# Expert networks in half-array tiles, with gate rows spread from DRAM

## The chip, the cores and the metric

The kernel runs on one core of one Trainium2 chip. The metric is the device time of one execution in microseconds (us), taken as the median of several runs. The engines are TensorE (PE in the profile, its weight loads PEld), VectorE (DVE), ScalarE (ACT), GpSimd (POOL) and SyncE (SP), whose queue issues the DMAs here.

## The reference

Input is `x` of 8 images, 64 channels, 16 by 16 pixels. Every layer adds its result to a running sum. A deformable 3x3 convolution and a second convolution come first; then, on 2048 tokens of 64 channels (8 images of 256 tokens): causal attention with 8 heads, a mixture of experts, a windowed attention, and a second mixture of experts. The two that the change touches, cut to what matters:

```python
# T: running sum, 2048 tokens x 64; y = layernorm(T) before each of them
# experts 2: E=8, hidden 256, top 2 of 8 experts per token
h = gelu(y @ W1[e] + b1[e]);           T += sum_e gate2[t, e] * (h @ W2[e] + b2[e])
# windowed attention over 16 tokens (needs its own layernorm), then
# experts 3: E=16, hidden 128, top 2 of 16
h = silu(y @ w1[e]) * (y @ w2[e]);     T += sum_e gate3[t, e] * (h @ w3[e])
```

All experts are computed for all tokens; `gate2` and `gate3` are zero but for a token's two best experts.

## The kernel before, in words

It is written engine by engine, one instruction stream each, with semaphores between them, and every stream has its order written out by hand. Tokens lie in 16 tiles of 128; four tiles make a chunk `c` of 512 tokens (`CHUNK`, `CW`). The stages in order are the convolutions, 64 attention steps (`scores`, `normalise`, with the fills of `attention_fills`), 64 steps of experts 2 and 64 steps of experts 3.

Layernorm output is kept as two float32r numbers, high and low part, whose sum is y. `Y2` holds both beside each other (64 + 64 columns), `transpose_y` turns them, and `ln_evac` puts them into `YTs`: partitions 0 to 63 the high part, 64 to 127 the low part, columns the tokens. The first-layer weights are split the same way: `WH` and `WL`, each with the same 64 rows twice. So two float32r matmuls of 128 rows, one with `WH` and one with `WL` (lines 1608 and 1659), give the full-precision product for 128 hidden units and 512 tokens.

Experts 2: step n makes one bank of 128 hidden units (L1608); ScalarE applies Gelu (L743) into `hid`; two steps later four float32 matmuls (L1627), one for each 128 tokens, take `hid` as the stationary operand and 64 columns of `W2` as the moving one, so that outputs have tokens on partitions. Line 1622 first puts the bias `b2` into the banks. Four experts (`UNIT`) of one chunk share two banks; `combine` (L1168) multiplies them by the gates, which are then plain per-token numbers, and GpSimd adds the four experts up by halving (`fold_unit`, `fold`, L513) and adds to `T` (L516).

Experts 3: each step makes two banks (L1659), ScalarE applies Silu to one (L753), VectorE multiplies by the other (L1258), and L1644 makes the output as above.

All other TensorE work of these stages (transposes of y, small projections for gates and window attention, the window sums, result transposes) is a "fill": `FIRST_FILLS` and `SECOND_FILLS` say after which step each comes, and they share one bank, number 7, which must be free (`misc_free`) before the next. VectorE does the layernorms (`ln_center`, `ln_variance`, `ln_out`), the gates (`take_logits`, `top_first`, `top_second`, `top_gate`), the window attention and most evacuations of bank 7; GpSimd also raises to powers (`ln_power`, `top_power`, `z_power`).

## Time and profile before

| what | value |
|---|---|
| median of 3 runs | 520.0 us (518.88 to 523.47) |
| profiled execution | 519.7 us, its span 517.9 us |
| TensorE clock granted, mean | 0.98 |
| PE busy | 476.3 us (92%) |
| VectorE busy | 360.5 us (70%) |
| ScalarE busy | 266.5 us (51%) |
| GpSimd busy | 170.8 us (33%) |
| the chain that ended last | PE 70%, DVE 20%, ACT 4%, issue 4% |

The span runs from the first to the last instruction; 1.8 us of the execution lie outside it. A float32 matmul stands in the profile as two records, a float32r matmul or a transpose as one. Durations of matmuls overlap, so what one costs is read from the distance between starts.

### The profile page before, as it was taken

The numbers are of one execution on the slowest core, as the hardware profiler recorded it, in microseconds if no ns is written. First come the engines' busy times: TensorE is split into PE (matmuls) and PEld (weight loads), VectorE is DVE, ScalarE is ACT, GpSimd is POOL, SyncE is SP. The second block draws the span as 40 slices with busy tenths as digits, with TensorE's granted clock in tenths as the row PEclk, the third lists the DMA queues.
The fourth block names the chain that finished last, engine by engine and source line by source line (L and its number), as shares of the span: only waits on it lengthen the run. The fifth ranks groups of instructions, "written<-read, shape, count | busy, mean of one in ns | idle before, by whom it ended". The sixth has DMA issues, their size and how long they took to land.

```text
span 517.9 us, 9531 instructions
## 1 busy us (share of the span) xinstructions
PE 476.3 (92%) x3406; PEld 408.0 (79%) x3406; DVE 360.5 (70%) x1050; ACT 266.5 (51%) x631; POOL 170.8 (33%) x217
## 2 busy tenths in 40 slices
PE   2998999959889999999999999999999989989994
PEld 2686787724449898899998998999999878878893
DVE  3288777368857768979797544366577998786844
ACT  1478666521328887888897544444443223322330
POOL 4800000001314493671133324033354434434332
PEclk9999999979979999999999999999999999999997
DMA  8200000000120303000000000000000000000000
GB/s 194 104 2 1 2 1 1 1 0 1 34 47 3 82 4 80 1 1 1 2 2 2 1 1 1 1 1 1 1 1 1 0 3 1 0 14 9 1 11 10
DMA packets 5458, 8.14 MB, mean 16 GB/s; under 512 B 2850, under 2 KB 4514, under 8 KB 4900
## 3 DMA queue, kind: packets, MB, share of 16 engines
q1 hardware_dynamic: 5268, 7.43, 5.9%
q8 instruction: 27, 0.44, 0.4%
q14 instruction: 19, 0.16, 0.1%
q10 hardware_dynamic: 144, 0.11, 0.1%
HBM read 7.01 MB, written 0.52 MB: 15 GB/s over the span
## 4 chain that ended last, share of the span: by engine, by line
PE 70%; DVE 20%; ACT 4%; issue 4%; DMA 1%; SPq 0%; DVEq 0%; ACTq 0%
PE PS L1659 11%; PE PS L1627 10%; PE PS L1644 9%; PE PS L1368 6%; PE PS L1608 6%; PE PS L1384 6%; PE PS L1532 4%; PE PS L1544 3%; DVE M L934 2%; PE PS L1329 2%; PE PS L1560 2%; PE PS L1561 2%; PE PS L1472 2%; ACT score_arena L721 2%; PE PS L1476 1%
## 5 line engine op out<-in xcount | busy, mean ns | idle before, releaser
L513 POOL TENSOR_TENSOR pr<-pr 128x512 f32<-128x512 f32 (+2 forms) x70 | 67.2, 961 | 108.6 <-DVE pr L1032 37.2
L753 ACT ACTIVATE VV<-PS 128x512 f32<-128x512 f32 x64 | 38.2, 597 | 86.8 <-PE PS L1659 86.8
L1627 PEld LDWEIGHTS PS<-wk,hid 128*128 128x128 f32 x512 | 66.6, 191 | 6.4 <-ACT hid L743 1.2
L1644 PEld LDWEIGHTS PS<-wk,hid 128*128 128x128 f32 x512 | 66.9, 191 | 5.6
L743 ACT ACTIVATE hid<-PS,wk 128x512 f32<-128x512 f32 x64 | 43.8, 687 | 49.2 <-PE PS L1608 49.2
L1627 PE MATMUL PS<-wk,hid 128*128 128x64 f32 x512 | 63.9, 268 | 0.7 <-ACT hid L743 0.7
L1644 PE MATMUL PS<-wk,hid 128*128 128x64 f32 x512 | 64.1, 268 | 0.0
L721 ACT ACTIVATE score_arena<-score_arena,nmx 128x128 f32<-128x128 f32 (+1 forms) x128 | 56.9, 447 | 13.6 <-DVE nmx L1127 13.0
L1258 DVE TENSOR_TENSOR hid<-VV,PS 128x512 f32<-128x512 f32 x64 | 43.8, 686 | 23.2 <-PE PS L1659 16.7
L1659 PE MATMUL PS<-YTs,WH 128*128 128x512 f32 x128 | 57.6, 450 | 1.9 <-DVE hid L1258 1.8
L1659 PE MATMUL PS<-YTs,WL 128*128 128x512 f32 x128 | 50.5, 395 | 0.0
L662 ACT ACTIVATE st_mem<-PS 128x512 f32<-128x512 f32 x72 | 36.5, 615 | 21.6 <-PE PS L1384 21.6
L887 DVE TENSOR_TENSOR prod<-hats 128x768 f32<-128x768 f32 x48 | 42.5, 951 | 0.1
L1532 PE MATMUL PS<-YTs,QH 128*128 128x128 f32 (+1 forms) x128 | 38.3, 323 | 0.0
L1544 PE MATMUL PS<-cst,score_arena 128*128 128x128 f32 x192 | 33.0, 280 | 4.7 <-ACT score_arena L721 4.2
L1384 PEld LDWEIGHTS PS<-cst,prod 128*128 128x128 f32 x288 | 31.3, 141 | 7.1 <-issue 3.5
L1384 PE MATMUL PS<-cst,prod 128*128 128x128 f32 x288 | 34.1, 275 | 2.8 <-DVE prod L887 1.9
L1168 DVE TENSOR_TENSOR pr<-PS,gate 128x512 f32<-128x512 f32 x48 | 30.8, 684 | 7.6 <-PE PS L1627 6.4
L1532 PE MATMUL PS<-YTs,QL 128*128 128x128 f32 (+1 forms) x128 | 36.0, 282 | 0.0
L490 POOL TENSOR_TENSOR lnst<-lnst,cst 128x4 f32<-128x4 f32 x16 | 16.3, 1022 | 55.5 <-DVE lnst L977 55.3
L1368 PE MATMUL PS<-st_mem,U 128*64 128x256 f32 x288 | 33.5, 383 | 0.0
L1019 DVE TENSOR_TENSOR QL<-PS,QH 128x512 fp32r<-128x512 f32 x32 | 22.0, 689 | 13.7 <-ACT QH L698 13.7
(225 smaller groups left out, 1065.4 us busy)
## 6 DMA issues: line engine op xcount, KB each, us to landing
stage<-in_wexp SPq DMA_DIRECT2D x6, 512.0 KB, 5.9
wk<-in_w SPq DMA_DIRECT2D x1, 1032.0 KB, 8.5
wa<-in_wat SPq DMA_DIRECT2D x1, 768.0 KB, 6.8
cst<-in_consts SPq DMA_DIRECT2D x1, 580.0 KB, 6.7
X<-in_x SPq DMA_DIRECT2D x2, 256.0 KB, 5.3
out<-X SPq DMA_DIRECT2D x16, 32.0 KB, 1.9
wc<-in_w SPq DMA_DIRECT2D x2, 183.5 KB, 6.2
score_arena<-in_wcv SPq DMA_DIRECT2D x2, 144.0 KB, 6.5
```

Source lines behind the costliest of these rows:

```text
L513: step(nc.gpsimd.tensor_tensor(buf[:, :, 0:width], buf[:, :, 0:width], buf[:, :, width:2 * width], ALU.add))
L721: ins = nc.scalar.activation(PR[:, s % 3, cols], MS[:, s % 3, cols], ACT.Exp, bias=nmx[:, s % 3, qt:qt + 1], scale=-1.0, accum_out=rsum[:, ...
L743: nc.scalar.activation(hid[:, n % 3], PS[:, n % 3, :], ACT.Gelu, bias=wk[:, W128["b1"]][:, e2:e2 + 1]).then_inc(gelu_done, 1)
L887: nc.vector.tensor_tensor(prods[unit % 2][:, b].rearrange("p k (a b) -> p k a b", a=HH), hk[:, 0].unsqueeze(3).to_broadcast([P, TRIPLE, HH ...
L1258: nc.vector.tensor_tensor(hid[:, n % 3], sil[:, n % 2], PS[:, (2 * n + 1) % 3, :], ALU.mult).then_inc(prod3_done, 1)
L1368: ins = mm(PS[h * C:(h + 1) * C, 5 + j % 2, 0:S], U[:, 4 * j + 2 * qt + h, k * C:(k + 1) * C], ST[:, v % ST_TAPS, h, qt], start=(k + qt == ...
L1384: ins = nc.tensor.transpose(PS[:, T_BANKS[m % 6], (2 * qt + pt) * P:(2 * qt + pt + 1) * P], prods[i // TRIPLE % 2][:, 2 * pt + h, k % TRIP ...
L1532: ins = mm(PS[:, s % 2, cols], w[:, a % 2, g, qt * P:(qt + 1) * P], YTs[:, a * S:a * S + (qt + 1) * P], start=(r == 0), stop=(r == 1))
L1544: ins = nc.tensor.transpose(PS[:, 3 + v % 2, k * P:(k + 1) * P], PR[:, v % 3, k * P:(k + 1) * P], ident)
L1627: ins = mm(accumulator(u, q, e % UNIT), hid[:, v % 3, q * P:(q + 1) * P], wk[:, W128["w2_2"]][:, r * C:(r + 1) * C], start=False, stop=(v ...
L1644: ins = mm(accumulator(u, q, e % UNIT), hid[:, v % 3, q * P:(q + 1) * P], wk[:, W128["w3"]][:, e * C:(e + 1) * C], start=True, stop=True)
L1659: ins = mm(PS[:, (2 * n + a) % 3, :], w[:, 1 + a, e * P:(e + 1) * P], YTs[:, c * CW:(c + 1) * CW], start=(k == 0), stop=(k == 1))
```

## The change

1. Output products of the experts. The stationary operand is now the 64 columns of `W2` or `w3`, the moving one is all of `hid` (512 tokens). Two experts are worked on as a pair: one writes PSUM partitions 0 to 63, the other 64 to 127 of the same bank (two 64-column tiles of the array). Outputs have channels on partitions and tokens along the bank. A pair of one chunk is a unit: 16 of experts 2, 32 of experts 3.
2. Input products. Three float32r products with 64 rows each (high by high, low weight by high y, high weight by low y) take the place of two with 128 rows; the two members of a pair use rows 0 to 63 and 64 to 127 (`split_pair`). For this a second transposed copy `YX` with the halves swapped is made: `Y2` gets a third block, `zB` and `zD` are its transposes.
3. Gates. Since tokens now run along the bank, the gate row of an expert must stand on 64 partitions. `gate_turn` turns the gates of a chunk (fills `tB`, `tD`), ScalarE copies them to `gate_rows`, SP stores them in DRAM, and for every unit SP reads the two rows back, each to 64 partitions (`gate_wide`, four slots).
4. Sums. `combine` handles one bank per unit (for experts 2 it also adds `b2`), GpSimd adds it to `acc` with one instruction, and once for each chunk and layer `token_sum` (fills `fC`, `fE`) turns the sum back to tokens and adds both halves; VectorE adds that to `T`.
5. Moves. Most evacuations of bank 7, the rounding to the high part and the output copies go from VectorE to ScalarE, the scaling by 1/sigma in these stages from VectorE to GpSimd. The bias matmuls go. `hid` has four slots in the room of `stage`. A step (q in experts 2, r in experts 3) now does a pair, so there are 32 of each. Fills and side work are put at new steps.

```diff
+            def split_pair(banks, m, tiles, c):
+                cs = slice(c * CW, (c + 1) * CW)
+                for k, (w, ys) in enumerate(((WH, (YTs, YX)), (WL, (YTs, YX)), (WH, (YX, YTs)))):
+                    for i in range(2):
+                        hs = slice(i * C, (i + 1) * C)
+                        ins = mm(PS[:, banks[i], :], w[hs, m, tiles[i] * P:(tiles[i] + 1) * P], ys[i][hs, cs], start=(k == 0), stop=(k == 2))
+                return ins
+            def first_out(q):
+                u, ht = divmod(q, 2)
+                if ht == 0 and u >= 3:
+                    pe.wait_ge(combined, u - 2)
+                pe.wait_ge(gelu_done, 2 * q + 2)
+                for i in range(2):
+                    r = tile2(u, 2 * ht + i)
+                    ins = mm(PS[i * C:(i + 1) * C, OUT_BANKS[u % 3], :], wk[:, W128["w2_2"]][:, r * C:(r + 1) * C],
+                             hid[:, (2 * q + i) % 4], start=(ht == 0), stop=(ht == 1))
+                ins.then_inc(out2_done, 1)
+            for q in range(2 * UNITS2):
...
+                if q >= 2:
+                    pe.wait_ge(gelu_done, 2 * q - 2)
...
+                split_pair([HID_BANKS[(2 * q + i) % 4] for i in range(2)], 0, [tile2(u, 2 * ht + i) for i in range(2)], c).then_inc(hid2_ready, 1)
+                if q >= 1:
+                    first_out(q - 1)
+                for what in FIRST_FILLS.get(q, ()):
+                    more(what)
+            for r in range(UNITS3):
...
+                for a in range(2):
+                    if r == 0:
+                        pe.wait_ge(gelu_done, 4 * UNITS2 - 1 + a)
+                    elif a == 0:
+                        pe.wait_ge(silu_done, 2 * r)
+                    else:
+                        pe.wait_ge(prod3_done, 2 * r)
+                    split_pair([HID_BANKS[2 * i + a] for i in range(2)], 1 + a, [2 * p + i for i in range(2)], c).then_inc(hid3_ready, 1)
+                if r >= 1:
+                    second_out(r - 1)
```

The gate path, on SP, TensorE and VectorE:

```diff
+            for u in range(UNITS2 + UNITS3):
+                m, c, p = unit_of(u)
+                if p == 0:
+                    E = (E2, E3)[m]
+                    sp.wait_ge(misc_free, FILL[("tB", "tD")[m], c] + 1)
+                    sp.dma_start(gate_store[m, c, 0:E], gate_rows[0:E, c % 2]).then_inc(gate_stored, 16)
+                    sp.wait_ge(gate_stored, 16 * (4 * m + c + 1))
+                if u >= WIDE:
+                    sp.wait_ge(combined, u - WIDE + 1)
+                for i in range(2):
+                    sp.dma_start(gate_wide[i * C:(i + 1) * C, u % WIDE, :],
+                                 gate_store[m, c, 2 * p + i:2 * p + i + 1, :].to_broadcast([C, CW])).then_inc(gate_spread[u % WIDE], 16)
+                if u >= UNITS2 + PAIRS3 and p == STORE_AT:
+                    store(c - 1)
...
+                dve.wait_ge(gate_spread[u % WIDE], 32 * (u // WIDE + 1))
+                if u >= 2:
+                    dve.wait_ge(acc_added, added(u - 1))
+                to = weighted[:, u % 2] if p else acc[:, c % 2]
...
+            def gate_turn(name, c):
+                m, E = (0, E2) if name == "tB" else (1, E3)
+                pe.wait_ge(gate_ready, 4 * m + c + 1)
+                take(name, c)
+                for q in range(CHUNK):
+                    ins = mm(PS[0:E, 7, q * P:(q + 1) * P], gate[:, m, 4 * c + q, 0:E], ident, start=True, stop=True)
+                ins.then_inc(misc_filled, 1)
+            def token_sum(name, c):
...
+                for q in range(CHUNK):
+                    ins = mm(PS[:, 7, q * C:(q + 1) * C], acc[:, c % 2, q * P:(q + 1) * P], c_("halves"), start=True, stop=not late)
```

The fills at their new steps:

```diff
+FIRST_FILLS = {0: (("zB", 2),), 1: (("tB", 0),), 2: (("tB", 1),), 4: (("tB", 2),), 5: (("yB", 3),), 6: (("gB", 3),), 7: (("zB", 3),),
+               10: (("fC", 0),), 13: (("yC", 0),), 14: (("pC", 0),), 16: (("tB", 3),), 18: (("wC", 0),), 19: (("fC", 1),),
+               21: (("yD", 0),), 22: (("gD", 0),), 23: (("yC", 1),), 24: (("pC", 1),), 25: (("zD", 0),), 26: (("fC", 2),),
+               28: (("wC", 1),), 29: (("tD", 0),), 31: (("yD", 1),)}
+SECOND_FILLS = {0: (("gD", 1),), 1: (("yC", 2),), 2: (("pC", 2),), 3: (("zD", 1), ("fC", 3)), 5: (("wC", 2),), 6: (("tD", 1),),
+                8: (("yD", 2),), 9: (("gD", 2),), 10: (("zD", 2),), 11: (("yC", 3),), 12: (("pC", 3),), 13: (("tD", 2), ("fE", 0)),
+                14: (("oT", 0),), 15: (("wC", 3),), 19: (("yD", 3),), 20: (("gD", 3),), 21: (("zD", 3), ("fE", 1)), 22: (("oT", 1),),
+                23: (("tD", 3),), 27: (("fE", 2),), 29: (("oT", 2),)}
```

In ScalarE's stream of experts 2, `y_high` (which waits for GpSimd's scaling) stands after the seventh Gelu (n = 6), then after n = 25, 41, 45 and 60.

## Rows read from the trace of the kernel before

**Rows 1.** The page, its second part: GB/s in 40 slices of 12.9 us.

```profile
GB/s 194 104 2 1 2 1 1 1 0 1 34 47 3 82 4 80 1 1 1 2 2 2 1 1 1 1 1 1 1 1 1 0 3 1 0 14 9 1 11 10
```

**Rows 2.** Stages: us, then PE, PEld, DVE, ACT, POOL busy (count), clock, DMA.

```profile
141.00:282.20 141.20, 133.41 (x1053) 121.99 (x1053) 110.15 (x435) 111.33 (x369) 59.45 (x89) 0.98 0.10 23
282.20:379.30 97.10, 95.63 (x702) 88.94 (x701) 51.24 (x139) 46.73 (x68) 33.16 (x35) 1.00 0.01 1
379.30:509.50 130.20, 125.53 (x829) 110.82 (x827) 101.84 (x218) 38.75 (x66) 53.64 (x57) 1.00 0.02 4
509.50:517.90 8.40, 0.81 (x4) 0.29 (x2) 3.25 (x6) 0.00 (x0) 0.00 (x0) 0.61 0.07 16
```

**Rows 3.** The chain that ended last, in order of time: start, us, what.

```profile
311.44 0.84 PE PS L1627 x8
312.80 0.84 PE PS L1627 x8
...
397.85 0.84 PE PS L1644 x8
398.69 0.98 PE PS L1659 x4
399.67 0.84 PE PS L1644 x8
```

**Rows 4.** Timeline of PE: float32r matmuls of 512 columns, and one fill.

```profile
342.64 0.61 PE L1459 MATMUL PS<-cst,Y 128*128 128x128 f32 x4
343.01 0.47 PE L1608 MATMUL PS<-YTs,WH 128*128 128x512 f32 x1
...
379.33 0.48 PE L1659 MATMUL PS<-YTs,WH 128*128 128x512 f32 x1
379.65 0.40 PE L1659 MATMUL PS<-YTs,WL 128*128 128x512 f32 x1
379.89 0.39 PE L1659 MATMUL PS<-YTs,WH 128*128 128x512 f32 x1
```

**Rows 5.** Timeline: float32 matmuls, in 64-column tiles (128*64) and in the whole array.

```profile
83.46 2.36 PEld L1368 LDWEIGHTS PS<-st_mem,U 128*64 128x64 f32 x24 [0.17 <-issue]
83.46 2.81 PE L1368 MATMUL PS<-st_mem,U 128*64 128x256 f32 x24
86.20 2.84 PE L1384 MATMUL PS<-cst,prod 128*128 128x128 f32 x24
...
132.61 7.13 PE L1316 MATMUL PS<-cst 128*128 128x512 f32 x16
```

**Rows 6.** Timeline of PE: float32r matmuls of 288 columns in 64-row tiles.

```profile
25.88 0.29 PE L1356 MATMUL PS<-DH,GL 64*128 64x288 f32 x1
25.99 0.29 PE L1356 MATMUL PS<-DL,GH 64*128 64x288 f32 x1
26.01 0.29 PE L1356 MATMUL PS<-DH,GL 64*128 64x288 f32 x1
26.12 0.29 PE L1356 MATMUL PS<-DL,GH 64*128 64x288 f32 x1
```

**Rows 7.** Groups of DVE instructions from 379.3 us on: count, busy, mean ns.

```profile
L1258 DVE TENSOR_TENSOR hid<-VV,PS 128x512 f32<-128x512 f32 x64 | 43.8, 686 | 23.2 <-PE PS L1659 16.7 <-issue 3.8 <-ACT VV L753 2.4
L1168 DVE TENSOR_TENSOR pr<-PS,gate 128x512 f32<-128x512 f32 x34 | 21.8, 683 | 2.3 <-PE PS L1644 1.2 <-PE PS L1627 1.1
L998 DVE CAST YTs<-PS 128x512 fp32r<-128x512 f32 x5 | 3.4, 682 | 0.0
```

**Rows 8.** Timeline at the start of experts 2: chunk 3's layernorm.

```profile
291.54 0.17 DVE L977 TENSOR_SCALAR lnst<-lnst 128x4 f32<-128x4 f32 x1
...
291.79 1.01 POOL L490 TENSOR_TENSOR lnst<-lnst,cst 128x4 f32<-128x4 f32 x1 [3.38 <-DVE lnst L977]
```

**Rows 9.** The page: two groups of ACT instructions.

```profile
L743 ACT ACTIVATE hid<-PS,wk 128x512 f32<-128x512 f32 x64 | 43.8, 687 | 49.2 <-PE PS L1608 49.2
...
L662 ACT ACTIVATE st_mem<-PS 128x512 f32<-128x512 f32 x72 | 36.5, 615 | 21.6 <-PE PS L1384 21.6
```

**Rows 10.** The page: DMA issues, KB each, median us to landing.

```profile
out<-X SPq DMA_DIRECT2D x16, 32.0 KB, 1.9
...
rw<-in_rows ACTq DMA_DIRECT2D x1, 103.0 KB, 4.0
```

**Rows 11.** Timeline of the end.

```profile
509.66 1.29 DVE L1168 TENSOR_TENSOR pr<-PS,gate 128x512 f32<-128x512 f32 x2 [1.20 <-PE PS L1644]
...
513.37 0.42 DVE L1251 COPY X<-PS 128x256 f32<-128x256 f32 x1 [0.78 <-PE PS L1503]
513.82 2.38 SPq L413 DMA_DIRECT2D out<-X  x4
```

## What the change will do to the time

> **What bounds the kernel now.** I read the stages first [rows 2]. TensorE is busy for 95.6 of the 97.1 us of experts 2 and for 125.5 of the 130.2 us of experts 3; VectorE for 51.2 and 101.8. The clock is granted in full (1.00, the 2.4 GHz level) in both. The chain that ended last says the same: it walks from one TensorE step to the next, every 1.36 us in experts 2 and every 1.82 us in experts 3 [rows 3]. A step's output part takes 0.84 us: eight records, each waiting for a weight load of 128 columns, though it streams only 64. Then the input part: a float32r matmul of 512 columns starts 0.234 us after the one before it, 0.31 us where it follows the float32 ones [rows 4]. So 64 x 1.36 = 87 us and 64 x 1.82 = 116 us are these steps; fills, bias matmuls and a few waits make the other 10 and 14 us. The profiled execution is 519.7 us for a span of 517.9, against a median of 520.0; I sum against the span and add 1.8 us.
>
> **Output products.** A float32 matmul is two records, and one record of 512 columns takes 7.13/16 = 0.44 us, less its tail 0.427, thus two 2.4 GHz cycles for a column [rows 5]. A pair has two matmuls, four records: 1.7 us if one after another, no better than now (two steps, 1.68 us). Do the column tiles overlap? L1368 is this form: 24 records of 256 columns, 0.213 us each by that rate, would be 5.1 us; they took 2.74 us to the next group's start [rows 5]. So two run at once: 12 x 0.216 = 2.59 us, and 0.15 us is the change of tiling at the ends. A pair's output is then 2 x 0.432 = 0.86 us.
>
> The Trainium skill speaks against this here (TensorE: Matmul & The Clock Gate, Part 3, The mechanism): a weight load overlaps running matmuls only where its row group differs, and column tiles share all rows. By it the four 64-column loads of a pair would stand on the path. The trace disagrees: the 24 loads of L1368 lie inside its matmuls.
>
> **Input products.** Three double matmuls take the place of two single ones per member. In 64-row tiles L1356 shows two streams, each with a start every 0.13 us for 288 columns (0.12 by 2.4 GHz), interleaved 0.02 us apart [rows 6]; so two at once again. For 512 columns I take 0.234 us per double: 0.70 us for a pair, against four matmuls, 0.94 us, now.
>
> **Changes of tiling.** Each step goes from row tiles to column tiles and back. From the same rows I take 0.15 us for each change, 0.30 us a step (between 0.1, which is only the late start, and 0.5, if the first weights can't be loaded early).
>
> **TensorE, summed.** Experts 2: 0.70 + 0.86 + 0.30 = 1.87 us a step, x32 = 60 us (87 before). Experts 3: 1.40 + 0.86 + 0.30 = 2.57 us, x32 = 82 us (116 before). The fills grow. A transposing fill cost 0.37 us and more to the next start [rows 4]; with the change of tiling 0.55. In experts 2 there are 8 of these (4.4 us), 5 gate turns of eight records like 128-column transposes, 0.9 us each (4.5), 3 sums of eight 128-column loads, 0.95 (2.9), and 6 small ones (3.0): 15 us. In experts 3: 7 transposes, 3 turns, 4 sums, and 10 small ones: also 15 us. The bias matmuls go. TensorE alone thus needs 75 and 97 us.
>
> **Experts 2, what is late next.** ScalarE: 64 x 0.687 = 44 us of Gelu [rows 9], 12 bank copies at 0.6 like L662 [rows 9], 5 roundings and two tanh: 55 us of 80, busy but not the bound; a step's two Gelus (1.4 us) must end in the 1.87 us until TensorE's output part, so a copy between them costs some tenths unless a fill lies there too. One wait is plain: the seventh Gelu is followed by a rounding that needs chunk 3's layernorm. L977 ends at 291.7 us, the power on GpSimd at 292.8 [rows 8], the scaling (new there, about 0.75) at 293.6. ScalarE would reach this place at about 291.6, and the eighth Gelu and TensorE's output part queue behind it: some 2.5 us. Later, chunk 0's and chunk 1's second layernorms end about 1 us behind the fills that need them, and the Gelu table comes at the start: 4 us together. 75 + 2.5 + 4 = 81 us, against 97.1.
>
> **Experts 3, what is late next.** VectorE. A step has two products (0.686 each) and one combine of the same size [rows 7]: 2.1 us with gaps. Of its 101.8 us now, products and combines are 65.6; of the other 36.2 us the copies out of bank 7, the scalings, the roundings, the final halving and one layernorm (12 us) leave this engine or stage; 5 sums add 2.1 us. That leaves 26 us, and about 100 short waits between dependent ones make it 31. All but 0.5 us of it lies in steps 0 to 22. The second input pair of a step waits for both products of the step before, so a step lasts as long as the longer of TensorE (2.57 + fill) and VectorE (2.1 + side work). Taken step by step, VectorE is the longer in 13 of the first 23 (up to 5.0 us at r = 4), and their sum is 83.5 us, where TensorE alone needs 72. The last nine take 25.4. With the last output part (1 us) and the start (a table load and the first products, 2 us) that is 112 us. For chunk 3 the gate row takes a store (1.9) and a broadcast (under 4.0) [rows 10] after its copy at r = 23, and its combine stands at r = 25: up to 2 us late, I take 1.5. 113.5 us, against 130.2.
>
> **Gate rows.** 256 KB a unit, each 2.6 to 3.5 us: 75 to 100 GB/s. The first slice of the kernel moved 194 GB/s [rows 1], and four slots run ahead, so I cost it at nothing beyond the above. If a unit's landing took longer than a step, all of it would show.
>
> **Elsewhere.** Attention gets two more fills with their evacuations on VectorE (0.55 and 0.68) and three more 256-column copies; both engines are near their bound there (133.4 and 110.2 of 141.2 [rows 2]), so +2 us (0 to 3). The end has 8.4 us now [rows 2, 11]: two combines, a halving and an addition on VectorE, a transpose, a copy, 2.4 us of stores. It becomes one combine (0.7), fourteen records of the late sum (1.8), one addition, transpose, copy, stores: 7.1 us. GpSimd has one addition per unit in place of three instructions: less than now.
>
> **Sum.** 282.2 + 2 + 81 + 113.5 + 7.1 = 485.8, +1.8 = 487.6; I say 488 us.
>
> **Rivals.**
> (a) The side work is hidden better: more TensorE time overlaps the long VectorE turns, and tiling changes cost 0.1. 282 + 70 + 100 + 7 + 2 = 461; halfway, 472. For: the longer-of-two sum lets nothing carry over between steps.
> (b) The opposite: VectorE's side work and ScalarE's copies don't overlap TensorE's but come on top, because hand-ordered streams wait for each other. Experts 3: 97 + 31 = 128; experts 2: 86; 282 + 2 + 86 + 128 + 7 + 2 = 507. For: each step has four handovers and only one step of slack.
> (c) Weight loads in column tiles don't hide, the rule above: 4 x 0.13 us by the busy time of a load in L1368 [rows 5], 64 steps: +33 us at most, near 520; only if the streams' overlap in L1368 doesn't carry over to 512 columns.
> By the Trainium skill's figure for a load (columns over 1.2 GHz; TensorE: Matmul & The Clock Gate, LDWEIGHTS) the estimate would be 0.21 us a step and 501 us.
> (d) Slower: the 64-row tiles don't run at once on 512 columns, or wait for each other's banks. Then 96 pairs cost 3 x 0.234 = 0.70 us more, +67 us: 555. It decides from 0.35 us per pair, half of that, where the gain of 32 us is gone. Against: L1356's two streams, in different banks as here.
> (e) Slower too: the broadcasts don't come in time. Did the two of a unit land one after another at 4.0 us, 48 x 8 us would hold the stages for 384 us in place of 195; the sign turns at 4.7 us a unit. Against: that row's DMA ran beside 194 GB/s of others.
>
> **How the numbers follow.** A measurement of this kernel tells 1% (5 us) from no change. Forecast, 479 to 498: 0.55. (a), under 479: 0.17. (b), 498 to 514.8: 0.14. (c) 0.04, (d) 0.05 and (e) 0.05, of which 0.04 falls within 1% and 0.09 beyond it, with other mishaps counted in; that leaves 0.01, given to faster. Faster by over 1%: 0.87; within: 0.04; slower: 0.09. The range leaves out the far ends of (a) and the cases from 514 on: 468 to 510.
>
> **What would show it.** L1659's and L1608's successors should come in couples within 0.02 us, couples 0.23 us apart; the output records in couples 0.43 us apart; a late step of experts 3 (r = 24 to 30) about 2.6 us. Experts 2 should end near 365 us and experts 3 near 479 us. ScalarE should sit for GpSimd after the seventh Gelu for about 2 us. In experts 3 TensorE should wait for VectorE's products at r = 1 to 5 and 9 to 11. VectorE should wait for a DMA only around r = 25. The forecast is wrong if couples are not couples, if a change of tiling costs more than 0.3 us, or if combines wait for DMAs throughout.

## The result, and the profile after

The changed kernel takes 501.4 us (median of 4 runs, 500.19 to 502.53) where the kernel before takes 519.55 (4 runs, 518.88 to 523.47): a ratio of 0.9635, with a 95% interval of 0.9581 to 0.9688. That is 18 us faster, inside the range of 468 to 510, but 13 us above the 488 us that I named and outside 479 to 498, to which I gave 0.55: it lies in the band of rival (b), which had 0.14. The profiled execution took 500.2 us for a span of 498.2 us.

The stages of the new kernel, in the columns of [rows 2] (us, then PE, PEld, DVE, ACT and POOL busy, clock, DMA):

```profile
141.00:284.06 143.06, 134.79 (x1060) 123.09 (x1060) 111.55 (x439) 111.41 (x369) 59.98 (x89) 0.98 0.10 23
284.06:371.90 87.84, 79.53 (x446) 35.59 (x445) 50.63 (x134) 52.05 (x86) 32.27 (x32) 0.98 0.18 59
371.90:489.80 117.90, 104.86 (x636) 53.10 (x634) 95.24 (x201) 45.21 (x84) 45.41 (x39) 0.99 0.23 70
489.80:498.20 8.40, 2.46 (x20) 2.06 (x18) 1.11 (x2) 0.38 (x1) 0.78 (x1) 0.76 0.08 16
```

Experts 2 went from 97.1 to 87.8 us and experts 3 from 130.2 to 117.9; attention is 1.9 us longer, the end as long as before. TensorE is idle for 8.3 of the 87.8 us (1.5 of 97.1 before) and for 13.0 of the 117.9 us (4.7 of 130.2 before). So part of the gain on TensorE turned into waits. The chain that ended last says the same (before: PE 70%, DVE 20%), and the slices of GB/s answer to [rows 1]: the broadcasts show from slice 24 on, at 22 to 117 GB/s, mostly 60 to 110, far below the 192 of the first slice.

```profile
GB/s 192 121 2 1 2 1 0 1 1 1 0 84 1 3 85 87 1 1 3 1 2 1 2 87 87 47 62 43 22 67 64 44 88 64 36 108 62 72 117 16
...
PE 54%; DVE 29%; issue 7%; ACT 5%; POOL 2%; DMA 1%; DVEq 0%; POOLq 0%; SPq 0%; ACTq 0%
```

One step of experts 2, from the timeline of PE. It answers to [rows 4 to 6]:

```profile
308.66 1.08 PE L1782 MATMUL PS<-stage,wk 128*64 128x512 f32 x4
309.67 0.50 PE L1771 MATMUL PS<-YTs,WH 64*128 64x512 f32 x1
309.67 0.50 PE L1771 MATMUL PS<-YX,WH 64*128 64x512 f32 x1
310.01 0.39 PE L1771 MATMUL PS<-YTs,WL 64*128 64x512 f32 x1
310.01 0.39 PE L1771 MATMUL PS<-YX,WL 64*128 64x512 f32 x1
310.24 0.39 PE L1771 MATMUL PS<-YX,WH 64*128 64x512 f32 x1
310.24 0.39 PE L1771 MATMUL PS<-YTs,WH 64*128 64x512 f32 x1
310.56 0.65 PE L1782 MATMUL PS<-stage,wk 128*64 128x512 f32 x2
```

The three products of a pair come in couples that start together, 0.23 us apart (0.34 after a change of tiling). From one output part to the next it is 1.90 us; a pair took two steps of 1.36 before [rows 3]. The output part takes 1.01 us with the change of tiling behind it, the input part 0.89 with its own. In experts 3 the same count gives 2.60 us (r = 24 to 26, 28, 30 take 2.59 to 2.61).

Three of the places where TensorE waits, from the timeline: the two longest waits and the one that I had forecast. First q = 21, the transpose of chunk 0's second layernorm:

```profile
337.15 0.41 DVE L1069 TENSOR_REDUCE lnst<-T 128x4 f32<-128x256 f32 x1
337.32 1.27 POOL L573 TENSOR_TENSOR pr<-pr 128x512 f32<-128x512 f32 x1 [0.82 <-DVE pr L1281]
337.60 1.27 DVE L1071 SCALAR_TENSOR_TENSOR Y<-lnst,T 128x256 f32<-128x256 f32 x1
...
339.89 0.42 DVE L1109 TENSOR_TENSOR Y<-Y 128x256 f32<-128x256 f32 x1
...
340.37 0.99 PE L1607 MATMUL PS<-cst,Y 128*128 128x128 f32 x4 [2.08 <-DVE Y L1109]
...
342.87 1.59 PE L1782 MATMUL PS<-stage,wk 128*64 128x512 f32 x4
```

VectorE does another chunk's statistics (L1069, L1071) ahead of the difference (L1109) that the transpose needs, and the instruction at L1071, which reads two SBUF operands, ends 0.28 us after GpSimd's addition ends: it takes 1.27 us beside it, where the same form takes 0.42 in other places. The transpose comes 2.08 us late, and then the output part at 342.87 takes 1.59 us in place of 1.08: the granted clock has fallen.

Second, experts 3 at r = 18:

```profile
442.77 1.02 POOL L524 TENSOR_TENSOR lnst<-lnst,cst 128x4 f32<-128x4 f32 x1 [3.15 <-DVE lnst L1082]
443.87 0.61 POOL L531 TENSOR_TENSOR Y<-Y,lnst 128x256 f32<-128x256 f32 x1
444.51 0.63 ACT L801 ACTIVATE Y<-Y 128x512 fp32r<-128x512 f32 x1 [3.28 <-POOL Y L531]
445.05 0.58 ACT L849 ACTIVATE VV<-PS 128x512 f32<-128x512 f32 x1
445.68 0.50 PE L1771 MATMUL PS<-YTs,WH 64*128 64x512 f32 x1 [2.56 <-ACT VV L849]
```

ScalarE stands at the rounding (L801), which waits for GpSimd, and the Silu that TensorE needs (L849) is queued behind it. Third, the place after the seventh Gelu that I forecast:

```profile
295.18 0.63 ACT L801 ACTIVATE Y<-Y 128x512 fp32r<-128x512 f32 x1 [0.92 <-POOL Y L531]
295.93 0.75 DVE L1281 SCALAR_TENSOR_TENSOR pr<-PS,wk,QH 128x512 f32<-128x512 f32 x1 [2.56 <-DMA QH<-gate_store]
296.44 1.08 PE L1782 MATMUL PS<-stage,wk 128*64 128x512 f32 x4 [1.01 <-ACT stage L831]
```

It costs TensorE 1.01 us. ScalarE sat for GpSimd for 0.92 us there, not for about 2. The second row is the only combine of both stages that is put down to a broadcast; no wait of TensorE is put down to that combine.

The end of the changed kernel, which answers to [rows 11]; the second row is the first two of the sixteen records of the late sum:

```profile
489.89 0.69 DVE L1284 TENSOR_TENSOR pr<-PS,QH 128x512 f32<-128x512 f32 x1 [0.66 <-PE PS L1793]
...
490.63 0.43 PE L1654 MATMUL PS<-cst,pr 128*128 128x64 f32 x2 [0.78 <-POOL pr L573]
...
492.67 0.42 DVE L1290 TENSOR_TENSOR T<-T,PS 128x256 f32<-128x256 f32 x1 [2.08 <-PE PS L1658]
...
494.09 2.39 SPq L434 DMA_DIRECT2D out<-X  x4
```

### The profile page after: what moved, and what is told of

The parts are those of the page before. It is cut to its first block, busy times and chain, and to the rows that moved or that the text cites. A ratio compares the mean times of both kernels' runs of the same rounds, so it can differ in the third digit from the quotient of the medians.

```text
span 498.2 us, 8873 instructions
## 1 busy us (share of the span) xinstructions
PE 442.7 (89%) x2982; PEld 299.8 (60%) x2982; DVE 352.8 (71%) x1029; ACT 278.7 (56%) x667; POOL 156.2 (31%) x189
## 4 chain that ended last, share of the span: by engine, by line
PE 54%; DVE 29%; issue 7%; ACT 5%; POOL 2%; DMA 1%; DVEq 0%; POOLq 0%; SPq 0%; ACTq 0%
PE PS L1771 9%; PE PS L1515 7%; PE PS L1531 6%; PE PS L1782 5%; PE PS L1695 4%; PE PS L1707 3%; DVE stage L1393 3%; PE PS L1793 2%; DVE M L1039 2%; PE PS L1476 2%; PE PS L1607 2%; DVE pr L1284 2%; PE PS L1620 2%; ACT score_arena L776 2%; PE PS L1723 2%
## 5 line engine op out<-in xcount | busy, mean ns | idle before, releaser
L1771 PE MATMUL PS<-YTs,WH 64*128 64x512 f32 x192 | 80.3, 438 | 5.8 <-DVE stage L1393 3.1
L573 POOL TENSOR_TENSOR pr<-pr 128x512 f32<-128x512 f32 x39 | 50.3, 1291 | 97.3 <-DVE pr L1284 65.0
L1771 PE MATMUL PS<-YX,WH 64*128 64x512 f32 x192 | 80.5, 438 | 0.0
L849 ACT ACTIVATE VV<-PS 128x512 f32<-128x512 f32 x64 | 35.2, 594 | 41.5 <-PE PS L1771 41.5
L1771 PEld LDWEIGHTS PS<-YTs,WH 64*128 64x128 f32 x192 | 35.8, 186 | 34.0 <-ACT VV L849 9.1
L1393 DVE TENSOR_TENSOR stage<-VV,PS 128x512 f32<-128x512 f32 x64 | 41.2, 682 | 16.6 <-ACT VV L849 8.9
L831 ACT ACTIVATE stage<-PS,wk 128x512 f32<-128x512 f32 x64 | 40.5, 684 | 17.9 <-PE PS L1771 17.7
L1771 PEld LDWEIGHTS PS<-YX,WH 64*128 64x128 f32 x192 | 35.8, 186 | 4.3
L1771 PE MATMUL PS<-YX,WL 64*128 64x512 f32 x96 | 38.1, 397 | 0.0
L1771 PE MATMUL PS<-YTs,WL 64*128 64x512 f32 x96 | 38.1, 397 | 0.0
L1782 PE MATMUL PS<-stage,wk 128*64 128x512 f32 x128 | 35.0, 626 | 3.4 <-ACT stage L831 3.4
L1793 PE MATMUL PS<-stage,wk 128*64 128x512 f32 x128 | 35.4, 631 | 0.5 <-DVE stage L1393 0.5
```

Of the source, the lines that this page charges most:

```text
L573: nc.gpsimd.tensor_tensor(acc[:, c % 2], acc[:, c % 2], weighted[:, u % 2], ALU.add).then_inc(acc_added, 1)
L831: nc.scalar.activation(hid[:, n % 4], PS[:, HID_BANKS[n % 4], :], ACT.Gelu, bias=wk[:, W128["b1"]][:, r:r + 1]).then_inc(gelu_done, 1)
L1393: nc.vector.tensor_tensor(hid[:, n % 4], sil[:, n % 2], PS[:, HID_BANKS[(2 * n + 1) % 4], :], ALU.mult).then_inc(prod3_done, 1)
L1771: ins = mm(PS[:, banks[i], :], w[hs, m, tiles[i] * P:(tiles[i] + 1) * P], ys[i][hs, cs], start=(k == 0), stop=(k == 2))
L1782: ins = mm(PS[i * C:(i + 1) * C, OUT_BANKS[u % 3], :], wk[:, W128["w2_2"]][:, r * C:(r + 1) * C], hid[:, (2 * q + i) % 4], start=(ht == 0) ...
L1793: ins = mm(PS[i * C:(i + 1) * C, OUT_BANKS[u % 3], :], wk[:, W128["w3"]][:, e * C:(e + 1) * C], hid[:, (2 * r + i) % 4], start=True, stop= ...
```

## The experiments

Each kernel changes the new kernel, or the reordered one (e3), in one thing; e11 takes several together. The table gives medians, and ratios to the kernel before run on the same chip (its median between 519.4 and 521.5 us in these sets; so a difference between two rows can differ by up to 2 us depending on whether it is taken from the medians or from the ratios, and both are given below where it matters). The last column is the length of experts 2 and of experts 3 in the profiled execution, each from its first input product to the first of the next stage, or to the last combine; steps that an edit doesn't touch repeat there within about 0.03 us. The start of experts 2 lay anywhere between 283.7 and 286.0 us in executions of kernels that are the same up to there (287.1 in e8), and such differences are in the medians. So small effects are read from the last column.

| kernel | median, us | ratio to before (95%) | experts 2, experts 3, us |
|---|---|---|---|
| the changed kernel | 501.4 | 0.9635 (0.9581 to 0.9688) | 87.8, 117.9 |
| e1, input products over 128 rows | 508.8 | 0.9749 (0.9702 to 0.9796) | 89.0, 124.4 |
| e2, no broadcasts | 500.5 | 0.9598 (0.9536 to 0.9660) | 86.3, 117.9 |
| e3, five moves in the order | 492.8 | 0.9439 (0.9389 to 0.9490) | 82.5, 114.3 |
| e4, both outputs in one column tile | 536.4 | one run | 109.2, 133.1 |
| e5, e3 and small GpSimd additions | 482.5 | 0.9281 (0.9236 to 0.9325) | 79.6, 108.5 |
| e6, e3 and evacuations back on VectorE | 497.9 | 0.9575 (0.9527 to 0.9623) | 82.5, 118.8 |
| e7, e3 and two further moves | 492.1 | 0.9450 (0.9404 to 0.9496) | 81.0, 114.6 |
| e8, e3 without the tie rule | 490.4 | 0.9419 (0.9372 to 0.9465) | 81.7, 112.2 |
| e9, e3 and additions in two pieces | 487.5 | 0.9358 (0.9317 to 0.9399) | 80.5, 112.3 |
| e10, e3 and additions in four pieces | 486.9 | 0.9346 (0.9303 to 0.9390) | 80.2, 110.9 |
| e11, e9 and three moves | 486.2 | 0.9330 (0.9293 to 0.9368) | 79.1, 111.7 |

### Parts of the change, one at a time

**e1: the input products as before, two matmuls of 128 rows for each bank.**

```diff
-                for k, (w, ys) in enumerate(((WH, (YTs, YX)), (WL, (YTs, YX)), (WH, (YX, YTs)))):
-                    for i in range(2):
-                        hs = slice(i * C, (i + 1) * C)
-                        ins = mm(PS[:, banks[i], :], w[hs, m, tiles[i] * P:(tiles[i] + 1) * P], ys[i][hs, cs], start=(k == 0), stop=(k == 2))
+                for i in range(2):
+                    for k, w in enumerate((WH, WL)):
+                        ins = mm(PS[:, banks[i], :], w[:, m, tiles[i] * P:(tiles[i] + 1) * P], YTs[:, cs], start=(k == 0), stop=(k == 1))
```

> The changed kernel with its input products made as before: two matmuls of 128 rows for each member, YTs alone as moving operand (the copy YX is still made, but not read). My theory: TensorE's own work is as summed and what is lost lies in waits between engines. Then a step of experts 2 goes from 1.90 to about 2.03 us (four matmuls 0.234 us apart and a late start, in place of three couples), one of experts 3 from 2.60 to about 2.95, where TensorE is the longer side; in total +8 to +15 us against the changed kernel, so 509 to 516. Rival, VectorE and the handovers set the steps throughout: within 3 us of the changed kernel, 499 to 504. Rival, row tiles cost as much in changes of tiling as they save: same or faster, under 501.

It took 508.8 us, 7.4 more than the changed kernel by the medians, 5.9 by the ratios, a little less than the 8 to 15 expected. The timeline of PE, one step:

```profile
330.29 0.50 PE L1770 MATMUL PS<-YTs,WH 128*128 128x512 f32 x1
330.62 0.40 PE L1770 MATMUL PS<-YTs,WL 128*128 128x512 f32 x1
...
331.09 0.40 PE L1770 MATMUL PS<-YTs,WL 128*128 128x512 f32 x1
331.42 1.08 PE L1781 MATMUL PS<-stage,wk 128*64 128x512 f32 x4
```

Four starts, 0.24 us apart and 0.33 behind the first, take the place of three couples. A bare step grew by 0.22 us in experts 2 (2.12) and by 0.47 in experts 3 (3.07): 32 x 0.69 = 22 us of TensorE's time, of which a third reached the end. The rest filled time in which TensorE had waited: experts 2 grew by 1.1 us only. The clock has a part in this: it is 1.00 throughout experts 2 of e1 (q = 22 takes 2.57 us against 3.65), and its fall costs the changed kernel 1.6 us there (see e2). So the 64-row tiles do what the diff says, and most of their gain is hidden by other waits.

**e4: both members' output products into the same 64-column tile.**

```diff
-                    ins = mm(PS[i * C:(i + 1) * C, OUT_BANKS[u % 3], :], wk[:, W128["w2_2"]][:, r * C:(r + 1) * C],
-                             hid[:, (2 * q + i) % 4], start=(ht == 0), stop=(ht == 1))
+                    ins = mm(PS[0:C, OUT_BANKS[u % 3], :], wk[:, W128["w2_2"]][:, r * C:(r + 1) * C],
+                             hid[:, (2 * q + i) % 4], start=(ht == 0 and i == 0), stop=(ht == 1 and i == 1))
```

(and the same at line 1793.)

> The changed kernel with both members of a pair writing their output to partitions 0 to 63, one on top of the other, in the same 64-column tile; the result is the sum of two ungated experts on the lower half and old data on the upper. Same matmuls, weights and waits. My theory: the two column tiles run at once, so here a step's output takes 1.72 in place of 0.86 us, +0.86 us a step; 64 steps give 55 us, less what now hides in waits: +40 to +55, 541 to 556. The output records should no longer come in couples. Rival, the matmuls of a pair are not truly parallel in the changed kernel (the couples are an artefact of the records): no change, 501.

It took 536.4 us, 35 more, and is slower than the kernel before:

```profile
332.99 1.93 PE L1782 MATMUL PS<-stage,wk 128*64 128x512 f32 x4
334.85 0.49 PE L1771 MATMUL PS<-YTs,WH 64*128 64x512 f32 x1
```

The output part takes 1.86 us to the next start, against 1.01 (308.66 to 309.67 above). Both of my figures for an output part, two at once and one after another, are now measured: the second costs 0.85 us more a step, and all of the gain hangs on the two column tiles running at once. The 54 us that this would be in 64 steps came down to 35, less than the 40 to 55 expected, again because some of it fell into waits. This is a single run, but the difference is far beyond what runs of one kernel differ by.

**e2: the 96 broadcasts and their waits left out.**

```diff
-                for i in range(2):
-                    sp.dma_start(gate_wide[i * C:(i + 1) * C, u % WIDE, :],
-                                 gate_store[m, c, 2 * p + i:2 * p + i + 1, :].to_broadcast([C, CW])).then_inc(gate_spread[u % WIDE], 16)
...
-                dve.wait_ge(gate_spread[u % WIDE], 32 * (u // WIDE + 1))
```

> The changed kernel without the 96 broadcasts of gate rows; combine multiplies by what lies in the slots, so the gates are left out of the result (the stores to DRAM and all else stay). My theory: the broadcasts are hidden, VectorE waited for them only at the first unit (2.6 us, with TensorE not yet waiting for it) and briefly at r = 25. So 0 to -1.5 us against the changed kernel: 499.5 to 502. Rival, the DMA traffic or late rows cost the missing gain: -5 us or more, 496 or less.

It took 500.5 us: 0.9 us less by the medians and 1.9 by the ratios, both inside the intervals. The trace says where it comes from: experts 3 takes the same 117.9 us, and the 1.6 us that experts 2 is shorter lie in q = 21 and 22 alone (4.64 and 2.44 us against 4.98 and 3.65), where the granted clock fell in the changed kernel and didn't in this one, after the same wait (2.08 us there, 2.09 here). So the broadcasts are hidden, rival (e) is out, and the 1.6 us are the price of the lower clock. In the changed kernel each of them landed in 2.9 us (the page's DMA issues, the row that answers to [rows 10]):

```profile
QH<-gate_store SPq DMA_DIRECT2D x96, 128.0 KB, 2.9
```

### Where TensorE waits

**e3: five moves in the hand-written order.** The rounding stands one Gelu later at two places and one Silu later at one; in units 9 and 14 of experts 2 the statistics of another chunk come behind the difference (`ln_low`, L1109) that a transpose needs.

```diff
-                if n in (6, 25, 41, 45, 60):
-                    y_high(*{6: (3, True), 25: (0, False), 41: (0, True), 45: (1, False), 60: (1, True)}[n])
+                if n in (7, 25, 41, 45, 61):
+                    y_high(*{7: (3, True), 25: (0, False), 41: (0, True), 45: (1, False), 61: (1, True)}[n])
...
-                if n in (1, 15, 20, 36):
-                    y_high(*{1: (2, False), 15: (2, True), 20: (3, False), 36: (3, True)}[n])
+                if n in (1, 15, 20, 37):
+                    y_high(*{1: (2, False), 15: (2, True), 20: (3, False), 37: (3, True)}[n])
...
                 if u == 9:
-                    ln_stats(1)
                     ln_low(0)
+                    ln_stats(1)
...
                 if u == 14:
-                    ln_stats(2)
                     ln_low(1)
+                    ln_stats(2)
```

> The changed kernel with five pieces of side work at other places in their engine's order: on VectorE ln_low ahead of ln_stats in the units 9 and 14, on ScalarE the roundings of chunk 3 and 1 in experts 2 one Gelu later (n = 7 and 61) and that of chunk 3 in experts 3 one Silu later (n = 37). Nothing else changes. My theory: TensorE waits there for work that is done or could be, and after two of these waits (2.1 and 2.6 us idle) its clock was granted at half for 3.4 us. Gains: about 1 at q = 4, 2.1 and the clock's 1.7 at q = 21, 1 to 2 at q = 31, 2 and the clock's 1.7 at r = 18: -7 to -10 us, so 491 to 494.5. Rival, a late step only moves the wait to the next handover: -3 us or less, 498 or more.

It took 492.8 us: 8.5 us less by the medians, 10 by the ratios. The stage of experts 2, by windows:

```profile
284.15:366.63 82.48, 77.81 (x445) 34.94 (x444) 50.56 (x133) 52.01 (x86) 30.44 (x30) 1.00 0.19 59
```

against 87.84 above: 5.4 us. The steps that changed are those that were touched: q = 4 from 3.95 to 2.87 us, q = 21 from 4.98 to 2.49, q = 22 from 3.65 to 2.44, q = 31 from 5.59 to 4.16; in experts 3 r = 18 from 6.05 to 3.43 and r = 19 from 4.77 to 3.74. One step took 0.84 us back, q = 23 (2.50 to 3.34). The work of every engine is the same, and the clock is 1.00 throughout the stage: q = 22 no longer runs at the lower level. The span fell to 489.3 us, by 8.9 of the 12.4 that it lay above my sum. Three roundings and two statistics that stood one place too early, and the clock that these idles took away, are thus worth most of the gap; but 6.5 us of waits in experts 2 were in my sum too, so this is not the same as closing the gap to the forecast.

**e7: two further moves: the search for the second expert stands one call later, behind what a transpose waits for.**

```diff
                 if u == 11:
-                    top_second(E3)
                     window_bias(1)
+                    top_second(E3)
...
                 if r == 10:
-                    top_second(E3)
                     ln_low(3)
+                    top_second(E3)
```

> e3_order with two more pieces of VectorE's side work moved: in unit 11 window_bias ahead of top_second (ScalarE's tanh, and the Gelus behind it, wait for it at q = 25), at r = 10 ln_low ahead of top_second (TensorE's fill at r = 11 waits for it). My theory: q = 25 lasts 3.99 us in place of about 2.5, r = 11 5.0 in place of about 3.6; -2 to -3 us against e3_order, 490 to 491. Rival, other handovers take up what is freed: within 1 us of e3_order.

492.1 us: no gain that can be told (-0.8 us by the medians, +0.6 by the ratios), where 2 to 3 were expected. The two moves fared differently. q = 25 went from 3.99 to 2.49 us and nothing took it back: experts 2 is 1.5 us shorter, which the medians don't show. r = 11 went from 5.04 to 3.60, but r = 12 from 3.15 to 4.83: the wait left r = 11 and reappeared a step later. e8, which takes work of VectorE away, shortens r = 11 by as much and r = 12 stays; so around r = 11 it is the amount of VectorE's side work that counts, and order alone doesn't remove it.

### VectorE's side work

**e6: seven evacuations of bank 7 in experts 3 back from ScalarE to VectorE.**

```diff
-                if n in (3, 7, 17, 21, 23, 39, 43):
-                    y_evac(*{3: ("yC", 2), 7: ("zD", 1), 17: ("yD", 2), 21: ("zD", 2), 23: ("yC", 3), 39: ("yD", 3), 43: ("zD", 3)}[n])
...
+                if r in (3, 8, 10, 11, 19, 21):
+                    ln_evac({3: "zD", 8: "yD", 10: "zD", 11: "yC", 19: "yD", 21: "zD"}[r], {3: 1, 8: 2, 10: 2, 11: 3, 19: 3, 21: 3}[r])
...
+                    ln_evac("yC", 2)
```

> e3_order with the seven evacuations of transposed y in experts 3 given back to VectorE (0.68 us each, right after the combine of the step). My theory: in the first 20 steps VectorE is the longer side, so most of 7 x 0.68 = 4.8 us shows: +3 to +6 us, 496 to 499. Rival, experts 3 is bound by TensorE and its fills: +1 us or less.

497.9 us: 5.0 us more by the medians, 7 by the ratios. Experts 2 stayed at 82.5 us, experts 3 went from 114.3 to 118.8. So this part of the change, which only moves work between engines, carries about 5 us, all of it in the stage where the copies stand. Not all of it is VectorE's time: the copies delay the fill of r = 21, TensorE stands still for 2.11 us, the clock falls behind that, and r = 22 takes 4.55 us in place of 2.96. About 1.6 of the 4.6 us are the clock.

**e8: the search for the second-best expert without the rule for ties,** three of VectorE's instructions and their waits fewer in each search.

```diff
-                step(nc.vector.tensor_tensor(key, src, wide(m, E), ALU.is_equal))
-                settle()
-                step(nc.vector.tensor_tensor(key, key, c_("desc")[:, E3 - E:E3].unsqueeze(1).to_broadcast([P, CHUNK, E]), ALU.mult))
-                settle()
-                step(nc.vector.tensor_reduce(mk, key, AX.X, ALU.max))
-                settle()
-                step(nc.vector.tensor_tensor(hot, key, wide(mk, E), ALU.is_equal))
+                step(nc.vector.tensor_tensor(hot, src, wide(m, E), ALU.is_equal))
```

> e3_order with the three instructions of each maximum that settle ties between experts left out (equal logits would give two experts; all else is computed). It shortens VectorE's side work by 18 instructions, about 5 us, in experts 3 and as many in experts 2. My theory: only the part in steps where VectorE is the longer side shows, r = 1, 3, 9, 10: -1.5 to -3 us, 490 to 491.5. Rival, no side work of VectorE is on the path: within 1 us.

490.4 us: 2.4 less by the medians, 1.0 by the ratios, and the intervals of the two kernels overlap. In the trace experts 3 is 2.0 us shorter (112.2) and experts 2 is 0.8. The total is as expected, the places are not: r = 1, 3, 9 and 10, which I had named, took the same time as in e3 within 0.02 us. The gain is in r = 11 (5.04 to 3.49 us), r = 23 (4.35 to 3.86) and q = 25 (3.99 to 3.23).

**e5: GpSimd's additions cut to 4 columns,** to take away what stretches VectorE's instructions.

```diff
-                nc.gpsimd.tensor_tensor(acc[:, c % 2], acc[:, c % 2], weighted[:, u % 2], ALU.add).then_inc(acc_added, 1)
+                nc.gpsimd.tensor_tensor(acc[:, c % 2, 0:4], acc[:, c % 2, 0:4], weighted[:, u % 2, 0:4], ALU.add).then_inc(acc_added, 1)
```

> e3_order with GpSimd's addition of each unit cut from 512 to 4 columns (the rest of the sums is left out of the result; waits and signals stay). In the changed kernel VectorE's instructions with both operands in SBUF were stretched while such an addition ran: L1071 to 1.27 us beside one, 0.42 without; over experts 3 about 10 us of stretching. My theory: this is a part of the VectorE time that holds TensorE in the steps r = 1 to 18, so -3 to -5 us against e3_order: 488 to 490. Rival, the stretching falls where VectorE has room: within 1.5 us of e3_order.

482.5 us: 10 us less by the medians, 8 by the ratios, twice what I expected; 8.7 us of it lie in the two stages. Groups of DVE instructions from 284 to 480 us, by form (count, busy, mean ns), first in e3:

```profile
L1284 DVE TENSOR_TENSOR pr<-PS,QH 128x512 f32<-128x512 f32 x31 | 21.2, 683 | 0.3 <-issue 0.3
L1071 DVE SCALAR_TENSOR_TENSOR Y<-lnst,T 128x256 f32<-128x256 f32 x9 | 5.3, 589 | 0.3
L1173 DVE TENSOR_TENSOR tg<-tg 128x64 f32<-128x64 f32 x8 | 4.7, 590 | 0.3
...
L1321 DVE COPY WX<-tg 128x4 f32<-128x4 f32 x4 | 2.5, 620 | 0.1
L1069 DVE TENSOR_REDUCE lnst<-T 128x4 f32<-128x256 f32 x9 | 3.7, 414 | 0.2
```

and in e5:

```profile
L1284 DVE TENSOR_TENSOR pr<-PS,QH 128x512 f32<-128x512 f32 x32 | 21.9, 685 | 2.0 <-issue 1.3 <-PE PS L1793 0.7
L1071 DVE SCALAR_TENSOR_TENSOR Y<-lnst,T 128x256 f32<-128x256 f32 x9 | 3.8, 424 | 0.3
L1173 DVE TENSOR_TENSOR tg<-tg 128x64 f32<-128x64 f32 x8 | 1.8, 225 | 0.3
...
L1321 DVE COPY WX<-tg 128x4 f32<-128x4 f32 x4 | 0.7, 172 | 0.1
L1069 DVE TENSOR_REDUCE lnst<-T 128x4 f32<-128x256 f32 x9 | 3.7, 416 | 0.2
```

A combine, which reads one operand from PSUM and one from SBUF, takes 683 ns in both; so does a sum over SBUF (L1069, 415 ns). Products of two SBUF operands and a plain copy from SBUF to SBUF are the ones that shrink, the small ones by a factor of three: they had stood behind a GpSimd addition. VectorE's busy time falls from 353.9 to 335.9 us in the whole kernel. The Trainium skill (SBUF — State Buffer, Who interferes with whom) says that the two engines share one pair of ports, that an instruction holds it for its whole length, and that a VectorE instruction with two SBUF inputs, or a copy in one of its two-port modes, contends where one with a single SBUF input otherwise doesn't; these rows agree with it. e5 also shortens GpSimd's own part, so how much of the 8 to 10 us is the stretching and how much an addition that is done sooner is not told apart by it; e9 and e10 are for that.

**e9 and e10: the same additions in two and in four pieces,** so that all work is done but no piece holds VectorE for long.

```diff
-                nc.gpsimd.tensor_tensor(acc[:, c % 2], acc[:, c % 2], weighted[:, u % 2], ALU.add).then_inc(acc_added, 1)
+                for at in range(0, CW, 256):
+                    ins = nc.gpsimd.tensor_tensor(acc[:, c % 2, at:at + 256], acc[:, c % 2, at:at + 256], weighted[:, u % 2, at:at + 256], ALU.add)
+                ins.then_inc(acc_added, 1)
```

> e3_order with each of GpSimd's additions of 512 columns split into two of 256; the result is unchanged. e5_small_add gained 10 us where 3 to 5 were expected. Theory one, stretching: a VectorE instruction that meets an addition ends with it, so shorter additions let it go earlier: L1071, L1173 and L1204 should show at most 0.9 us in place of 1.27 or 1.05, and the time falls by 2 to 4 us against e3_order, 489 to 491. Rival, queueing: what counted in e5 was GpSimd's own chain (powers, scalings and sums standing behind additions); then two pieces, which take no less together, gain nothing: 492 to 494.

> e3_order with each addition in four pieces of 128 columns, result unchanged. Theory one, stretching: as with two pieces and a little more, 488 to 490, unless the four together (0.35 to 0.5 us each) take so much longer that VectorE meets them more often. Rival, queueing: GpSimd's additions become longer by 0.3 to 0.7 us, so its chain is later and the time goes up by 1 to 3 us, 493 to 496.

487.5 and 486.9 us: 5.3 and 5.9 less than e3 by the medians, 4.2 and 4.8 by the ratios. By the stages it is 3.9 us for two pieces and 5.7 for four. In e9, from 284 to 480 us:

```profile
L1073 DVE SCALAR_TENSOR_TENSOR Y<-lnst,T 128x256 f32<-128x256 f32 x9 | 4.3, 478 | 0.3
L1175 DVE TENSOR_TENSOR tg<-tg 128x64 f32<-128x64 f32 x8 | 2.7, 339 | 0.3
```

These are L1071 and L1173 of e3, at 589 and 590 ns there; the longest L1073 takes 0.74 us, as theory one asked (at most 0.9). GpSimd's part becomes longer and not shorter (groups of POOL instructions, first e9 and then e10):

```profile
L574 POOL TENSOR_TENSOR pr<-pr 128x256 f32<-128x256 f32 x78 | 58.3, 768 | 80.4 <-DVE pr L1286 54.6 <-DVE pr L1283 25.7
```

```profile
L574 POOL TENSOR_TENSOR pr<-pr 128x128 f32<-128x128 f32 x156 | 70.2, 480 | 71.8 <-DVE pr L1286 47.0 <-DVE pr L1283 24.7
```

against 39 of 1290 ns, 50.3 us, in e3. An addition that is done later and a kernel that is faster: this tells the two readings of e5 apart. Of e5's 8.7 us in the stages, 3.9 (two pieces) and 5.7 (four) come without any addition done sooner, by cutting the instruction, at no change in the work. The medians don't tell four pieces from two. In the profiled executions the two stages of e10 are 1.8 us shorter than those of e9, and its end is 1.7 us longer, at a mean clock of 0.59 against 0.75: the late sum ran at the lower level (0.50 from 477.2 to 480.5 us).

**e11: e9, the moves of e7, and the gates of the third chunk found one step later.**

```diff
-                if r == 11:
-                    top_gate(2, E3)
...
+                    top_gate(2, E3)
```

> e9_two_pieces (the moves of e3_order and GpSimd's additions in two pieces) with the moves of e7_order2 and, so that r = 12 does not take back what r = 11 gains, top_gate of chunk 2 moved from r = 11 to r = 12. e7_order2 gained 1.5 us at q = 25 and 1.4 at r = 11 and gave 1.7 back at r = 12. Theory, each wait has one late step that can be named: -2 to -3 us against e9_two_pieces, 484.5 to 486. Rival, the waits only change places: within 1 us of 487.5.

486.2 us (485.18 to 486.86), ratio 0.9330: the fastest of all that computes everything, 1.4 us below e9, just short of the 484.5 to 486 expected. The intervals overlap, but the trace shows what the moves did: q = 25 went from 3.88 to 2.50 us, r = 11 from 4.57 to 3.25 and r = 13 from 6.12 to 5.60, while r = 12 rose from 3.17 to 4.47 in spite of the later `top_gate`. The two stages together are 2.0 us shorter, most of it the one step of experts 2. Against the changed kernel it is 3.1% of the time before, 16 us.

## Why the prediction came out as it did

The direction and TensorE's own part, term by term, held; the waits came out larger, and at other places, than I had them. Of the 12.4 us that the span (498.2) lies above my sum (485.8), each term has this much:

| term | forecast, us | measured, us |
|---|---|---|
| start of experts 2 | 284.2 | 284.06 |
| experts 2: bare steps | 60 | 32 x 1.90 = 61 |
| experts 2: fills | 15 | 16.8 |
| experts 2: waits | 2.5 + 4 | 10.2 |
| experts 3: TensorE alone | 97 | 100.1 |
| experts 3: waits above that | 16.5 | 17.8 |
| end | 7.1 | 8.4 |

- *Output products* ("two run at once", 0.86 us a pair): right, and e4 is the proof; in one tile it costs 0.85 us a step more. With the change of tiling I had 1.01, and it took 1.01.
- *Weight loads in column tiles*, rival (c): they hide, so the rule that the prediction named against it put no time on this kernel. Four loads of 0.13 us (132 to 137 ns each in the trace before; the row shown, 24 overlapping loads in 2.36 us, doesn't give it) on the path would have made a bare step of 1.90 + 0.52 = 2.4 us. In the new kernel the four loads of an output part end within 0.20 us of the first one's start, before the first matmul is done (the timeline of PEld):

```profile
442.04 0.20 PEld L1793 LDWEIGHTS PS<-stage,wk 128*64 128x64 f32 x4 [0.36 <-DVE pr L1284]
```

- *Input products* (0.70 us a pair) and *changes of tiling* (0.15 each): 0.89 us for an input part with one change, forecast 0.85. Rival (d) is out: the couples start together, and e1 gives the price of doing without them.
- *Fills* (and the bare steps, 0.03 us each, 1.0 in each stage): a mis-sized term. I had 0.55 us for a transpose with its changes of tiling, which took 0.57 to 0.60; a gate turn took 0.97 against 0.9, a sum 1.04 against 0.95. Of the small ones a window sum took 0.87, where I had 0.5 for each. Small each, but 3.7 us over both stages.
- *Experts 2, what is late next*: 3.7 us too little, the wait that I had most wrong. The wait after the seventh Gelu was named rightly and over-priced (1.0 us on TensorE against 2.5, as ScalarE comes there 2.7 us later than I had it). "About 1 us behind the fills that need them" was far too small for the later layernorms: q = 21 alone lost 2.5 us in its own step and 1.2 in the next (1.6 of these 3.7 by the clock), and q = 25 and q = 31 lost 1.5 and 2.1. I had counted the chain of that layernorm by its own instructions, and neither the other chunk's statistics queued between them nor their stretching. e3 moved them and took 5.4 us out of experts 2.
- *Experts 3* (83.5 + 25.4 by the longer of TensorE and VectorE): right in size, in part by luck. Waits came to 17.8 us, near my 16.5, and of the first 23 steps, forecast at 83.5 us and 2 for the start, 89.7 were measured. But the mechanism that I summed, input products that wait for VectorE's products of the step before, has only a small share. Of the 13.0 us for which TensorE is idle in this stage, 3.6 are such waits (seven of L1771 and one of L1793 for L1393); 4.4 are fills that wait for VectorE's side work, 2.4 are fills behind ScalarE's copies, and 2.6 is the wait for a Silu at r = 18. r = 4, my longest step at 5.0 us, took 2.61, and r = 2 had no wait either. VectorE is busy for 95.2 us, against 65.6 + 26 = 92 by my count, and r = 18 was not on my list at all: ScalarE's rounding waits for GpSimd there with a Silu behind it, 2.6 us. That is the mechanism that I had seen in experts 2 and not looked for in experts 3.
- *Late gate row at r = 25* (1.5 us): didn't happen. VectorE waited for a broadcast at the first unit only. Its combine stood 0.4 us behind its output part and steps 24 to 26 took 2.59 to 2.61 us.
- *Gate rows at nothing*: right (e2).
- *The end* (7.1 us): 8.4. Sixteen records and not fourteen, 0.22 us for a couple, in all 2.04 us from the first record to the addition, where I had 1.8, and handovers of 0.05 to 0.2 us between the other parts.
- *Attention* +2 us: +1.9.
- Rival (b), side work on top, 507 us: the time came out 13 us above my case and 6 below this one. Experts 2 took 87.8 us (86 by the rival, 81 by me), experts 3 117.9 (128 and 113.5). Its reason, each step's four handovers with little slack, is what e3 and e7 show.

Two things weren't in the sum at all: the stretching of VectorE's instructions behind GpSimd's (4 to 5 us by e9, on the reordered kernel), and the clock that falls after an idle (about 1.6 us at each of two places: 1.59 by e2 for the first, and at r = 19 its 4.77 us against 3.20 of bare step and fill, with no idle in it). The first could have been read from the trace before. Of its groups of DVE instructions from 282 to 509 us, by form, one shows it:

```profile
L1060 DVE TENSOR_TENSOR tg<-tg,cst 128x64 f32<-128x64 f32 x8 | 2.9, 362 | 0.3
L1064 DVE TENSOR_TENSOR tg<-tg 128x64 f32<-128x64 f32 x8 | 1.8, 224 | 0.3
```

Two products of the same size, one 1.6 times as long in the mean. I took VectorE's side work from such groups as if the surroundings would stay the same. The second couldn't be read from these two stages: the clock was 1.00 in both before, where TensorE's longest wait was 1.5 us.

What stays open: how far the last 3 us of e5 (8.7 in the stages, of which e10 has 5.7) are the rest of the stretching or the shorter addition.

## What to carry to other kernels

When TensorE's part of a step shrinks by a third, price what then comes last one step at a time, and walk each in-order stream for the pattern "waits for a slow chain, with the busiest engine's producer queued behind": moving five such waits by one place was worth half as much as the whole change. Read the smallest and the largest duration of a VectorE form beside its mean; if they differ threefold, a neighbour may be blocking it, and cutting the neighbour's instruction in two can help though it costs that engine time. A resource that looks risky (96 broadcasts) may be free and a rearrangement of matmuls may be mostly hidden: measure both by leaving one out.

## What the runs showed of the hardware

**The granted clock fell after short idles, and not always.** Windows of the changed kernel just behind the waits of q = 21 and r = 18, in the columns of the stages above:

```profile
341.00:343.50 2.50, 2.50 (x10) 1.12 (x10) 0.00 (x0) 1.11 (x2) 0.80 (x2) 0.50 0.00 0
...
446.50:449.50 3.00, 3.00 (x12) 1.05 (x10) 2.06 (x4) 1.08 (x2) 1.38 (x1) 0.50 0.22 81
```

TensorE stood still for 2.08 and 2.56 us and then worked at 0.50, the 1.2 GHz level, though it was busy all the time. In those stretches couples of input products start 0.42 us apart in place of 0.23. In e2, where TensorE stood still for 2.09 us at the same place, the clock stayed at 1.00 and q = 22 took 2.44 us in place of 3.65. In e6 it fell after 2.11 us at r = 21.

**A step has 0.34 us beyond its streams** (0.70 + 0.86 of 1.90): 0.15 behind the output part (1.01 us, where two couples at 0.432 us make 0.86), 0.10 between its first couple of input products and the second (0.34 and not 0.23 us) and 0.09 ahead of the output part (0.32). In e1, whose input products use all rows, the sum is the same (2.12 - 0.94 - 0.86 = 0.32). How much of it belongs to the tiles and how much to the change between float32 and float32r isn't told apart: [rows 4] has nearly the same 0.10 us without tiles (0.32 and not 0.24 us).

**VectorE and GpSimd.** A VectorE instruction of 0.17 to 0.42 us with two SBUF operands, or a copy within SBUF, took 0.9 to 1.5 us when a GpSimd addition of 1.27 us had begun shortly before it (L1071 1.27 us at 337.60, L1109 1.48 us at 317.43, 0.07 us behind the addition's start); a sum over one SBUF operand kept its 0.41 us; one with an operand in PSUM kept its 0.68 us.
